# RWKV time mix and mixture of experts on one core: both norms' row statistics move from VectorE to ScalarE, and the residual enters W_o's product as an identity matmul

## The reference

```python
def attn(x, ...):                        # x: 2 x 4096 x 256
    xx = shift(x) - x                    # the token before, minus x
    ...                                  # tanh products mix x and xx four ways: xw, xk, xv, xr
    r, k, v = xr @ W_r, xk @ W_k, xv @ W_v
    w = exp(-exp(time_decay + tanh(xw @ dw1) @ dw2))
    y = wkv6(r, k, v, w, u)              # S = w * S + k v^T over 4096 steps; y_t = r_t (S + u k v^T)
    mu  = mean(y, -1); var = mean(square(y - mu), -1)
    y = (y - mu) * rsqrt(var + 1e-5) * ln_g + ln_b
    return y @ W_o

def layernorm(x):
    m = mean(x, -1); v = var(x, -1)
    return (x - m) / sqrt(v + 1e-5)

x = layernorm(x + attn(x))
x = layernorm(x + moe(x))                # 32 experts, top 2, capacity 615 rows, F = 1024, exact gelu
```

## Time and profile before

| what | value |
|---|---|
| median of 3 runs | 2342.34 us (2333.91 to 2342.52) |
| the profiled execution's own time | 2343.03 us |
| its span, first to last instruction | 2341.3 us |
| mean granted TensorE clock | 0.922 |
| DVE busy over the span | 1834.2 us (78%) |
| PE busy over the span | 1938.1 us (83%) |
| POOL busy over the span | 1373.3 us (59%) |
| ACT busy over the span | 1059.1 us (45%) |
| bodies 1 to 15 of `time_mix` | about 150 to 1276 us |
| stage C of the last chunk alone | about 1276 to 1338 us |
| `experts` | about 1340 to 2281 us |
| `last_norm` | about 2287 to 2341 us |

### The profile page before, as it was taken

One profiled execution on the slowest core, in us unless ns is written; L12 is line 12 of the kernel. 1 busy time (PEld: TensorE's weight loads), 2 busy tenths in 40 slices (PEclk: granted clock), 3 DMA queues, 4 the chain that ended last, 5 costly groups with the idle time before them and its releaser, 6 DMA issues. The chain is left out here.

```text
span 2341.3 us, 33041 instructions
## 1 busy us (share of the span) xinstructions
PE 1938.1 (83%) x9894; PEld 1336.8 (57%) x9894; DVE 1834.2 (78%) x3157; ACT 1059.1 (45%) x1919; POOL 1373.3 (59%) x954
## 2 busy tenths in 40 slices
PE   5777888788777887877776299999999999999980
PEld 2333343333333333433332189999999999999970
DVE  2899999899999998999997266666666666666655
ACT  2233553345334543444432255555555555555546
POOL 3667787768777787678775224444444444454440
PEclk9889999899989998999886599999999999999995
DMA  6932111111112111111020144545454545455538
GB/s 163 220 87 64 46 46 54 47 54 36 51 47 58 29 51 42 58 29 49 31 69 20 58 122 121 122 121 120 120 120 122 120 120 121 120 123 122 124 57 287
DMA packets 172844, 209.00 MB, mean 89 GB/s; under 512 B 12796, under 2 KB 152480, under 8 KB 172768
## 3 DMA queue, kind: packets, MB, share of 16 engines
q1 hardware_dynamic: 112688, 143.09, 20.7%
q0 software_dynamic: 28672, 34.78, 8.6%
q10 hardware_dynamic: 31408, 30.33, 5.0%
HBM read 118.65 MB, written 75.53 MB: 83 GB/s over the span
## 5 line engine op out<-in xcount | busy, mean ns | idle before, releaser
L807 DVE TENSOR_TENSOR_SCAN S<-wT,S,vb 128x512 f32<-128x512 f32 x512 | 624.9, 1262 | 0.0
L1070 POOL TENSOR_TENSOR prod<-S,rT 128x2048 f32<-128x2048 f32 x128 | 536.8, 4198 | 148.0 <-DVE S L807 147.8
L1289 PE MATMUL up<-x_parts,w_parts 128*128 128x308 f32 x3072 | 464.2, 307 | 1.5 <-DVE x_parts L1402 1.5
L1304 PE MATMUL down<-w_parts,h_parts 128*128 128x512 f32 (+1 forms) x1280 | 452.4, 396 | 0.0
L1289 PEld LDWEIGHTS up<-x_parts,w_parts 128*128 128x128 f32 x3072 | 439.2, 189 | 4.1 <-issue 1.8
L1364 POOL TENSOR_TENSOR ye<-ye,weight 128x256 f32<-128x256 f32 (+1 forms) x160 | 197.7, 1235 | 379.9 <-DVE ye L1458 379.9
L1342 ACT ACTIVATE h_full<-up,b_now 128x616 f32<-128x616 f32 x256 | 198.6, 776 | 421.2 <-PE up L1289 409.6
L1372 POOL DMA_INDIRECT sums<-ye,sum_at x160 | 281.6, 1760 | 150.1 <-POOL ye L1364 140.0
L1445 DVE TENSOR_TENSOR h_parts<-h_full,h_parts 128x616 fp32r<-128x616 f32 x256 | 206.8, 808 | 193.1 <-ACT h_parts L1342 192.8
L1307 PE MATMUL down<-w_parts,h_parts 128*128 128x256 f32 (+1 forms) x1280 | 357.4, 279 | 0.0
L571 PE MATMUL vb<-v_stack,pick_v 128*128 128x512 f32 x512 | 216.7, 507 | 152.0 <-DVE S L807 151.8
(11 more groups left out here) (176 smaller groups left out, 2645.2 us busy)
## 6 DMA issues: line engine op xcount, KB each, us to landing
w_raw<-in_L_ffn_w_dram SPq DMA_DIRECT2D x64, 1024.0 KB, 8.8
expert_in_rows<-y_tok ACTq DMA_DIRECT2D x30, 652.5 KB, 9.1
xe<-expert_in_rows SPq DMA_DIRECT2D x32, 522.0 KB
v_stack<-v_parts SPq DMA_DIRECT2D x64, 256.0 KB, 4.5
x_tok<-in_L_attn_x_dram SPq DMA_DIRECT2D x16, 512.0 KB, 3.3
x_res<-in_L_attn_x_dram SPq DMA_DIRECT2D x16, 512.0 KB, 3.4
sums<-x_row SPq DMA_DIRECT2D x16, 512.0 KB, 2.9
rows<-sums SPq DMA_DIRECT2D x16, 512.0 KB, 5.5
```

Source lines behind the costliest of these rows:

```text
L807: dve.tensor_tensor_scan(line[:, 1:TC + 1], wT[:, par, half, :], vb[:, p % 2, g, :], line[:, 0:1], ALU.mult, ALU.add).then_inc(scanned, 1)
L1070: pool.tensor_tensor(prod[:, q % 2], S[:, q % RING, :, 0:TC], rT[:, par, half, None, :].to_broadcast([P, QUAD, TC]), ALU.mult).then_inc(pr ...
L1289: last = pe.matmul(up[:, f % 2, half, 0:HC], w1_parts[:, par, wp, k, f * P:(f + 1) * P], x_parts[:, par, xp, k, half * HC:(half + 1) * HC] ...
L1304: pe.matmul(down[0:m, (par * TILES + t) % 2, :, :], h_parts[:, 0, f, t * P:t * P + m], w2_parts[:, par, :, f, :], start=f == 0, stop=False)
```

## The change

- The first norm. ACT's drain of the turned rows into `y_tok` was one activation of 512 columns for two row tiles; now it is one of 256 for each, and each also writes its row sum to `total`. At slot 8 ACT makes minus the mean from it (L914 of the changed kernel), then four `Square` activations (L918) with that as bias, which write the sums of squared differences to `square`; their full output goes to a scratch tile that nothing reads. ACT's square root (slot 10) takes `square` with scale 1/C. DVE's `bn_stats` and `bn_aggr` go; its reciprocal stays.
- The residual. PE multiplies the identity by `x_res` into the same PSUM columns ahead of W_o's product (L535), so there are two more matmuls of 256 columns in each of slots 17 and 19. PE now waits for `x_res`.
- The second norm. ACT drains the sum into `x1` at slots 18 and 20 (L898, each two activations of 256 with a row sum) in place of DVE's addition, and so has the waits on the store and the scatter of the chunk before. At slot 21 it takes the squares as above. DVE keeps the reciprocal at slot 23.
- In `last_norm` a group's 512 rows lie as (p t): a partition holds four rows that follow each other in memory, one run of 4 KB, for loads and stores alike.

```diff
-        stats = sb("stats", [P, 2, TPC, 6])
-        mv = sb("mv", [P, 2, TPC, 2])
+        total = sb("total", [P, 2, TPC])
+        square = sb("square", [P, 2, TPC])
+        squares = sb("squares", [P, TPC, C])
...
-        C_AT = {"turn": 6, "stat1": 9, "root1": 10, "norm1": 12, "back": 14, "wo0": 17, "z0": 18, "wo1": 19,
+        C_AT = {"turn": 6, "stat1": 8, "root1": 10, "norm1": 12, "back": 14, "wo0": 17, "z0": 18, "wo1": 19,
...
-        LN1_AT = 2 * TPC + 1
-        X1_AT = LN1_AT + 2 * TPC + 1
+        LN1_AT = 1
+        X1_AT = LN1_AT + 1
...
                     if s == C_AT[f"wo{k}"]:
                         c_fill(i, 4 + k)
+                        if k == 0:
+                            pe.wait_ge(res_loaded, stage_value(i, 16, 16))
                         for t in range(2):
+                            pe.matmul(pc[:, t * C:(t + 1) * C], ident[:], x_res[:, 2 * k + t, :],
+                                      start=True, stop=False)
                             for h in range(NH):
                                 at = (2 * k + t) * P
                                 last = pe.matmul(pc[:, t * C:(t + 1) * C], yT[:, h, at:at + P],
-                                                 wo_sb[:, h, :], start=h == 0, stop=h == NH - 1)
+                                                 wo_sb[:, h, :], start=False, stop=h == NH - 1)
...
-            def statistics(src, which):
-                for t in range(TPC):
-                    dve.bn_stats(stats[:, which, t, :], src[:, t, :]).then_inc(s_dve, 1)
-
             def stage_c(i, par, s):
-                if s == C_AT["stat1"]:
-                    dve.wait_ge(c_drained, stage_value(i, NCF, 2))
-                    statistics(y_tok, 0)
-                    chain(i, TPC)
-                    dve.sem_inc(wait_carrier, 1)
-                    for t in range(TPC):
-                        dve.bn_aggr(mv[:, 0, t, :], stats[:, 0, t, :]).then_inc(s_dve, 1)
                 if s == C_AT["norm1"]:
                     invert(i, 0)
-                for k in range(2):
-                    if s == C_AT[f"z{k}"]:
-                        dve.wait_ge(c_full, stage_value(i, NCF, 5 + k))
-                        if k == 0:
-                            dve.wait_ge(res_loaded, stage_value(i, 16, 16))
-
-                            wait_from(dve, x1_stored, stage_value(i, 16, 0))
-                            wait_from(dve, scattered, stage_value(i, 16 * 2 * TPC, 0))
-                        dve.tensor_tensor(x1[:, 2 * k:2 * k + 2, :], pc[:].rearrange("p (t c) -> p t c", t=2),
-                                          x_res[:, 2 * k:2 * k + 2, :], ALU.add).then_inc(c_drained, 1)
-                if s == C_AT["stat2"]:
-                    dve.wait_ge(c_drained, stage_value(i, NCF, 6))
-                    statistics(x1, 1)
-                    chain(i, LN1_AT + TPC)
-                    dve.sem_inc(wait_carrier, 1)
-                    for t in range(TPC):
-                        dve.bn_aggr(mv[:, 1, t, :], stats[:, 1, t, :]).then_inc(s_dve, 1)
                 if s == C_AT["norm2"]:
                     invert(i, 1)
...
-                        act.activation(y_tok[:, 2 * k:2 * k + 2, :], pc[:].rearrange("p (t c) -> p t c", t=2),
-                                       ACT.Copy).then_inc(c_drained, 1)
+                        for t in range(2):
+                            ins = act.activation(y_tok[:, 2 * k + t, :], pc[:, t * C:(t + 1) * C], ACT.Copy,
+                                                 accum_out=total[:, 0, 2 * k + t:2 * k + t + 1])
+                        ins.then_inc(c_drained, 1)
+                    if s == C_AT[f"z{k}"]:
+                        act.wait_ge(c_full, stage_value(i, NCF, 5 + k))
+                        if k == 0:
+                            wait_from(act, x1_stored, stage_value(i, 16, 0))
+                            wait_from(act, scattered, stage_value(i, 16 * 2 * TPC, 0))
+                        for t in range(2):
+                            ins = act.activation(x1[:, 2 * k + t, :], pc[:, t * C:(t + 1) * C], ACT.Copy,
+                                                 accum_out=total[:, 1, 2 * k + t:2 * k + t + 1])
+                        ins.then_inc(c_drained, 1)
...
+                for which, (name, rows) in enumerate((("stat1", y_tok), ("stat2", x1))):
+                    if s == C_AT[name]:
+                        act.wait_ge(c_drained, stage_value(i, NCF, 2 + 4 * which))
+                        act.activation(minus_mean[:, which, :], total[:, which, :], ACT.Copy, scale=-1.0 / C
+                                       ).then_inc(mean_kept, 1)
+                        act.wait_ge(mean_kept, stage_value(i, 2, which + 1))
+                        for t in range(TPC):
+                            ins = act.activation(squares[:, t, :], rows[:, t, :], ACT.Square,
+                                                 bias=minus_mean[:, which, t:t + 1],
+                                                 accum_out=square[:, which, t:t + 1])
+                        ins.then_inc(squared, 1)
                 for which, name in enumerate(("root1", "root2")):
                     if s == C_AT[name]:
-                        act.wait_ge(s_dve, stage_value(i, NCH, (2 * TPC, LN1_AT + 2 * TPC)[which]))
-                        act.activation(rstd[:, which, :], mv[:, which, :, 1], ACT.Sqrt, bias=eps_col[:, 0:1]
-                                       ).then_inc(root_done, 1)
-                        act.activation(minus_mean[:, which, :], mv[:, which, :, 0], ACT.Copy, scale=-1.0
-                                       ).then_inc(mean_kept, 1)
+                        act.wait_ge(squared, stage_value(i, 2, which + 1))
+                        act.activation(rstd[:, which, :], square[:, which, :], ACT.Sqrt, bias=eps_col[:, 0:1],
+                                       scale=1.0 / C).then_inc(root_done, 1)
...
-            return dram[bass.ds(g * (GT * P) + first, GT * P), :].rearrange("(t p) c -> p t c", p=P)
+            return dram[bass.ds(g * (GT * P) + first, GT * P), :].rearrange("(p t) c -> p t c", t=GT)
```

More of the change, by code:

```diff
@@ L261, in time_mix @@
         s_dve = sem("s_dve")
+        squared = sem("squared")
         root_done = sem("root_done")
```

## The result

The changed kernel took **2377.3 us** (median of 4 runs, 2376.44 to 2384.21), the kernel before 2342.4 us (median of 4, 2333.91 to 2342.52) beside it. The medians differ by 35 us, where 40 had been forecast and 2342 to 2405 given as the range. The ratio over all the runs is 1.0165, 95% interval 1.0135 to 1.0194 (that of the medians alone is 1.0149): slower. The profiled execution of the changed kernel took 2377.36 us, its span is 2375.5.

What follows compares the result with a forecast made beforehand. ACT's lateness before DVE's second reciprocal was taken as the bound, not DVE's load. Bodies +37, body 15 -5.6, last stage C +9.7, `last_norm` -1: +40 on 2343 gives 2383 us, range 2342 to 2405.

Steps and rivals of the forecast that it cites:

- What bounds the body: Steady bodies: ACT's lateness before DVE's second reciprocal, a 0.82 us wait with 18 us of DVE work behind it.
- Rival 2: Steady bodies: DVE stays the bound, so the kernel gets faster, 2247 us or about 2295; chance 0.13.
- Rival 3: ACT's row sums: reading one out costs some 0.6 us, giving 2411 us; chance 0.13.
- Rival 1: Steady bodies: the added wait is swallowed, a body stays at 76.4 us, the kernel at 2343; chance 0.12.
- Reciprocal at A + 30.8: DVE's second reciprocal starts 30.8 us after A, PE's spread in pair 6, where it was 26.6: +4.2 us.
- PE's spread of pair 11: In each body, this PE step was to come 24.3 us after PE's spread in pair 6, 23.45 before.
- The identity matmuls: PE's extra residual matmuls at slots 17 and 19: 0.41 us each, four of them, +1.6 us per body.
- the squares: ACT's second-norm mean, squares and read-outs between the second exponential and the table load: 3.3 us, ends 2.5 and 3.7.
- The rest of the body: Reciprocal to end of pair 15 18.0 us, then 30.2 to the next A: body 79.0 against 76.4, +2.6.
- Body 15: The body without a stage A: PE waits for DVE and ACT has time, so -5.6 us.
- The last stage C: The final stage C, run alone with every step on the path: +9.7 us.
- `last_norm`: New row layout there: ACT sets the period, only first load and last store lie open; -1 us, ends -3 and 0.

Runs made afterwards that it cites:

- e1: Kernel before with the first norm's edits alone (drains of `y_tok` with sums, mean and squares on ACT): 2332.67 us, ratio 0.9978.
- e6: Changed kernel with the second norm's four squares taken twice in every chunk: 2417.07 us, ratio 1.0320 to the kernel before.
- e8: Changed kernel with the second norm's mean and squares of tiles 0 and 1 moved to slot 19: 2365.59 us, ratio 1.0096 to the kernel before.
- e11: Kernel before with the residual's identity matmuls alone; DVE copies where it added and keeps its statistics: 2362.44 us, ratio 1.0086.
- e12: e9 with ACT's drain of the first half of `x1` moved from slot 18 to 17: 2315.07 us, ratio 0.9892 to the kernel before.
- e9: Changed kernel with squares of tiles 0 and 1 early, DVE's second reciprocal behind pair 12, `y_sum` copied ahead of ACT's second exponential: 2325.97 us.
- e5: Changed kernel with ACT's copy of the first half of `y_sum` moved ahead of its second exponential: 2378.55 us, ratio 1.0158 to the kernel before.
- e4: Changed kernel with DVE's second reciprocal one slot later, behind pair 12: 2382.67 us, ratio 1.0179 to the kernel before.
- e3: Kernel before with the (p t) row layout of `last_norm` alone: 2340.64 us, ratio 1.0005.
- e7: Changed kernel with DVE's second reciprocal behind pair 12 and `y_sum` copied ahead of ACT's second exponential: 2355.62 us, ratio 1.0062 to the kernel before.

## Why the prediction was right, and where it was not

**What bounds the body: right.** The forecast went by the 0.82 us wait and not by DVE's 94%. e1, e6 and e8 bear it out, and e11 in kind. Rival 2 (DVE stays the bound, 2247 or 2295) is out: the 5 us of DVE work a body became idle time. Rival 3 is out too: a read-out takes 187 to 201 ns and not 600, and in the rows above it starts (741.78) 0.10 us before the end that the trace gives for its square. Rival 1, the swallowed wait, is out: the time is 34 us above it.

**Reciprocal at A + 30.8: right in sum (A + 30.82), by two errors that cancel.** PE's spread of pair 11 came at A + 25.43, not A + 24.3. The identity matmuls were put at 1.6 us and took 0.43 to 0.54 each, 1.9. The term left out is PE's 0.80 us wait for ACT's drain of `x1`, where DVE's addition had come in time; the prediction had the drains fit into ACT's idle time. e12 removes this wait from e9 and gains 0.89 us a body. On the other side the squares were priced at 3.3 us with ends 2.5 and 3.7 and took 2.3 (741.14 to 743.46), below the low end: the next square starts 0.09 us behind the start of a read-out, where 0.2 us each had been allowed, and a square costs less than a scaling. Groups of ACT, whole span, each shape apart:

```profile
L936 ACT ACTIVATE x_row<-x_row,offset,rstd 128x256 f32<-128x256 f32 x64 | 33.2, 590 | 0.5
...
L918 ACT ACTIVATE squares<-x_row,minus_mean 128x256 f32<-128x256 f32 x64 | 31.7, 497 | 0.5
...
L898 ACT ACTIVATE x_row<-pc 128x256 f32<-128x256 f32 x64 | 23.6, 375 | 14.9 <-PE pc L539 14.9
L898 ACT ACTIVATION_READ_ACCUMULATOR x_row<-pc 128x1 f32 x64 | 12.9, 201 | 0.0
...
L918 ACT ACTIVATION_READ_ACCUMULATOR squares<-x_row,minus_mean 128x1 f32 x64 | 12.0, 187 | 0.0
```

Two operands per partition cost 590 ns, one 497: 93 ns, the figure that the prediction took from the Trainium skill ("ScalarE: Activation LUTs", "What ACT_TABLE_LOAD costs"). The trace agrees. With the 6 us that the prediction works out from it, the forecast would have been 2377, though its meeting the measured time is chance, as the errors named here are larger.

**The rest of the body: right in sum.** From the reciprocal to the spread behind pair 15 it took 17.87 us (18.0), from there to the next A 30.64 and, in the body behind, 29.53 (30.2 both). A body measured 78.8 for 79.0; by the marks 2.29 more than before for 2.6. That 18 us stretch was called DVE's own, and e5 shows that it is. What the prediction did not see is what lies right under it: e4 laid PE's path through `y_sum` bare. It reaches through in the changed kernel as well: in three of the 14 bodies the clock behind PE's stop was 0.50, DVE waited 0.5 to 0.9 us for the logits, and the mark stood 19.1 to 19.6 us behind the reciprocal, for 18.4 to 18.6 in the others.

**Body 15: wrong.** -5.6 was forecast, -0.4 came. The step that failed is "PE waits for DVE and ACT has time". It was read from one wait of PE, and it took DVE for the bound of the whole body. DVE's busy time in body 15 fell from 65.7 to 61.3 us, and DVE then waited for PE, 4.99 us in three waits of the changed kernel, where it waited 0.83 before (0.53 and 0.30):

```profile
1262.96 1.30 DVE L778 TENSOR_TENSOR vb<-vb,kT 128x512 f32<-128x512 f32 x2 [1.42 <-PE vb L577]
...
1278.82 1.30 DVE L778 TENSOR_TENSOR vb<-vb,kT 128x512 f32<-128x512 f32 x2 [1.53 <-PE vb L577]
...
1299.06 0.29 DVE L732 TENSOR_TENSOR logits<-pc,gate_bias 128x128 f32<-128x128 f32 x1 [2.04 <-PE pc L554]
```

The first of these spreads stands on PE behind a product sum that waits for POOL, and that wait is the same in both kernels, before and then after:

```profile
1230.24 1.94 PE L581 MATMUL ypsum<-prod,sum_y 128*32 128x512 f32 x8 [4.60 <-POOL prod L1070]
```

```profile
1260.26 1.94 PE L587 MATMUL ypsum<-prod,sum_y 128*32 128x512 f32 x8 [4.63 <-POOL prod L1068]
```

Both stand 21.0 us behind the mark that opens the body. In the kernel before, DVE took its first statistics while PE stood there. What makes PE late at the other two waits was not tested.

**The last stage C: right in kind, wrong in size.** +9.7 forecast, +5.0 measured (50.2 for 45.2). Here the two norms' steps stand bare. The first squares step took 2.3 and the root followed: +1.65 for 2.6; W_o's product with the residual +2.6 for about 4; the second statistics +0.4 for 1.3; the drains of `y_tok` and what leads up to them +0.4 for 1.7. Read-outs and squares were priced too high by the same errors as in the body; the identity matmuls were not (+1.5 and +0.9 for 1.8 and 0.8).

**`last_norm`: right in that it hardly counts.** -1 forecast; the rest of the execution differs by -0.4 us in the table, and e3 finds no difference that the runs can tell.

## What to carry to other kernels

An engine busy 94% of the time need not be the one to relieve. Here it waited 0.8 us for the release behind which its longest unbroken stretch begins: look at what released that stretch, and price every instruction put ahead of it. When the removal of a wait gives nothing, the next wait's length tells what a second move would free: two moves that each measured as nothing gave 22 us together. Work that moves to another engine needs its order there chosen anew: with three moves and one number the same change went from a ratio of 1.0165 to the kernel before to one of 0.9892.

## What the runs showed of the hardware that was not expected

- The row sum of an activation is an instruction of its own (`ACTIVATION_READ_ACCUMULATOR`), 187 to 201 ns busy, but it overlaps its neighbours: squares with a read-out follow each other every 0.49 us with 497 ns of their own, and 0.09 us of that lies between the start of the read-out and the next square.
- DVE's addition of a 128x512 PSUM tile and an SBUF tile and its plain copy of the same tile take the same (680 ns before, 0.69 in e11).
- PE's granted clock over the 5 us behind PE's stop, the idle stretch that ends with the product sum or the transposes of `x1`: 0.50 to 0.72 behind all 14 stops of 4.1 to 4.2 us (after); 0.66 to 0.68 behind nine of 14 stops of 2.6 to 2.7 us and 1.00 behind five (e7); 1.00 behind 13 of 14 stops of 1.7 to 1.8 us and 0.66 behind one (e9). The length of the stop alone doesn't tell which it will be. Where the clock fell in e7, DVE waited 1.2 to 2.5 us longer; in e5, with the same stops, it didn't wait at all, as its own 18 us were the longer path.
- Four runs of 1 KB a partition against one of 4 KB, 16 groups: no difference in the time that the runs can tell, though the store's issue fell from 0.38 to 0.34 us. ACT's own work sets the pace there, 2.72 us a group before, so this says little of the transfers themselves.
